# Edge block of a two-layer convolution kernel: the 512x512 fusion product as three float32r products of split operands

## The reference

```python
# layer 0
q, k, v = h @ wq.T, h @ wk.T, h @ wv.T            # 5x5 depthwise and 8x8 grouped convolutions of these are heads too
out = relu(q) . ((v, 1)^T relu(k)) / normaliser
x = batch_norm(proj_kernel @ out) + x
# layer 1, the edge block
E = [sobel, |laplace|, max of two |diagonals|, gradient]       # 3x3 stencils of x, four maps
feat = gelu(batch_norm(w_branch[e] @ E[e]))                     # 4 x 128 channels = 512
pooled = feat.mean(over pixels)
att = sigmoid(w_att2 @ gelu(w_att1 @ pooled))                   # one gate for each channel and image
z = w_fuse @ (feat * att) + b_fuse                              # the fusion product
zn = (z - mean_c(z)) / sqrt(var_c(z) + eps)
out = gelu(zn * ln_gamma + ln_beta) + x
```

## Time and profile before

| | us |
|---|---|
| median of 3 runs (lowest, highest) | 5002.34 (5001.51, 5005.30) |
| profiled execution: its time | 5005.31 |
| its span, first to last instruction | 5003.5 |
| TensorE busy (share) | 4718.9 (94%) |
| VectorE, ScalarE, GpSimd busy | 2836.0 (57%), 2173.3 (43%), 1253.1 (25%) |
| mean granted TensorE clock | 0.973 of full speed |
| matmuls of the fusion product (line 1142), busy | 454.4 in 1024 instructions |

### The profile page before, as it was taken

One profiled execution on the slowest core, in us unless ns is written; L12 is line 12 of the kernel. 1 busy time (PEld: TensorE's weight loads), 2 busy tenths in 40 slices (PEclk: granted clock), 3 DMA queues, 4 the chain that ended last, 5 costly groups with the idle time before them and its releaser, 6 DMA issues. The chain is left out here.

```text
span 5003.5 us, 68940 instructions
## 1 busy us (share of the span) xinstructions
PE 4718.9 (94%) x23784; PEld 3647.3 (73%) x23784; DVE 2836.0 (57%) x3927; ACT 2173.3 (43%) x3927; POOL 1253.1 (25%) x1030
## 2 busy tenths in 40 slices
PE   8999999999999999999999999589989998998968
PEld 7887888888878878888888788466546645654623
DVE  3354454454454444544544544279679949967975
ACT  3343343333333433333333333046556646646665
POOL 2341432433423414424333234000020021002003
PEclk9999999999999999999999999799999999999979
DMA  6675685676666756756766666767446646745613
GB/s 186 214 268 188 222 280 192 217 251 210 230 212 218 257 193 231 271 195 221 239 207 231 217 217 228 249 218 250 153 166 221 226 139 202 255 143 179 192 48 119
DMA packets 480190, 1044.92 MB, mean 209 GB/s; under 512 B 40368, under 2 KB 90160, under 8 KB 477616
## 3 DMA queue, kind: packets, MB, share of 16 engines
q1 hardware_dynamic: 479920, 1040.98, 62.1%
HBM read 665.02 MB, written 375.82 MB: 208 GB/s over the span
## 5 line engine op out<-in xcount | busy, mean ns | idle before, releaser
L786 POOL TENSOR_TENSOR toeplitz<-taps 128x512 f32<-128x512 f32 x768 | 918.5, 1224 | 993.9 <-PE bank L465 909.5
L465 PEld LDWEIGHTS bank<-toeplitz,columns 128*128 128x128 f32 x8192 | 954.4, 192 | 13.9
L465 PE MATMUL bank<-toeplitz,columns 128*128 128x128 f32 x8192 | 955.7, 275 | 0.0
L380 PE MATMUL bank<-x_hi,w_hi 128*128 128x512 f32 x1536 | 609.7, 397 | 15.5 <-DVE x_lo L635 15.5
L382 PE MATMUL bank<-x_lo,w_hi 128*128 128x512 f32 x1536 | 600.4, 391 | 0.0
L381 PE MATMUL bank<-x_hi,w_lo 128*128 128x512 f32 x1536 | 598.7, 390 | 0.0
L1451 POOL TENSOR_TENSOR centred<-centred,x_out 128x512 f32<-128x512 f32 x128 | 164.8, 1321 | 1708.2 <-ACT centred L1258 1708.2
L1116 PE MATMUL bank<-edge,w_branch 128*128 128x512 f32 x1024 | 480.4, 619 | 88.0 <-ACT edge L1209 88.0
L1102 PE MATMUL bank<-att_hi,w_proj_hi 128*128 128x512 f32 x1024 | 436.2, 426 | 62.2 <-DMA att_lo<-att_dram 50.5
L455 PE MATMUL bank<-loaded,toeplitz 128*128 128x256 f32 x2048 | 485.8, 379 | 7.8 <-POOL toeplitz L786 7.8
L635 DVE TENSOR_TENSOR x_lo<-x_sb,x_hi 128x1536 fp32r<-128x1536 f32 x128 | 251.9, 1968 | 399.6 <-ACT x_hi L511 399.6
(11 more groups left out here) (123 smaller groups left out, 6994.1 us busy)
## 6 DMA issues: line engine op xcount, KB each, us to landing
x_sb<-in_x_tiled SPq DMA_DIRECT2D x128, 1024.0 KB, 6.1
tiles_dram<-tiles SPq DMA_DIRECT2D x128, 867.0 KB, 7.0
loaded<-tiles_dram SPq DMA_DIRECT2D x256, 433.5 KB, 5.6
inverse<-inverse_dram SPq DMA_DIRECT2D x256, 256.0 KB, 7.9
att_dram<-out_hi SPq DMA_DIRECT2D x256, 256.0 KB, 4.2
att_dram<-out_lo SPq DMA_DIRECT2D x256, 256.0 KB, 5.9
att_hi<-att_dram SPq DMA_DIRECT2D x64, 1024.0 KB, 7.6
att_lo<-att_dram SPq DMA_DIRECT2D x64, 1024.0 KB, 10.0
```

The source lines that it names most:

```text
L380: nc.tensor.matmul(banks[t][:, :], wh, xh, start=(k == 0), stop=False)
L465: last = nc.tensor.matmul(bank[:, v * M:(v + 1) * M], columns[:, h % 2, t - T_K, v + b, a * HT:(a + TO) * HT], w[:, t, d, :], start=(d == ...
L786: last = nc.gpsimd.tensor_tensor(toeplitz[:, h % 2, t, :].rearrange("p (d o r) -> p d o r", o=HD, r=PL), tap, point, ALU.mult)
```

## The change

The fusion product is no longer made of float32 operands. `feat` is split, chunk by chunk, in a rounded part and a remainder: ScalarE rounds a 128x512 piece with a Copy into half 1 of `att_hi` (even chunks) or `att_lo` (odd chunks), four pieces a chunk (`round_feat`), VectorE subtracts for pieces 0 and 1 and GpSimd for pieces 2 and 3 (`split_feat`), writing `feat_lo` over `feat`. The gated weights are made as two parts: ScalarE writes `w_hi` with a Copy scaled by the gate, VectorE the remainder `w_lo`. For each of the four k, `fuse` now issues three float32r matmuls, wide x high, narrow x high and wide x low, instead of one float32 product. TensorE waits at m = 0 of each chunk for both subtracting engines. On SyncE, the load of half 1 of the next attention chunk moves from the drain to a place behind store 5 of the fusion, where it waits for the last fusion product of the image. GpSimd's residual additions of chunk j - 2 now stand behind its subtractions for chunk j + 1.

```diff
--- before.py
+++ after.py
@@ -832,7 +832,9 @@
         LAG = 3
         HALF = TILES // 2
         PIX = CR * W2
-        feat = sb("feat", [P, NE, N])
+        with nc.sbuf_tensor("feat", [P, NE, N], F32) as feat:
+            pass
+        feat_lo = ctx.enter_context(nc.sbuf_tensor("feat_lo", [P, NE, N], F32R))
         xb = sb("xb", [P, KT, XR * W2])
         work = sb("work", [P, 3, XR * W])
         with nc.sbuf_tensor("mean_w", [P, P], F32) as mean_w:
@@ -840,7 +842,7 @@
         sobel_h = sb("sobel_h", [P, 2, CR, W])
         sobel_v = sb("sobel_v", [P, 2, CR, W])
         lap_sq = sb("lap_sq", [P, 2, CR, W])
-        with nc.sbuf_tensor("w_image", [P, KT, C], F32) as w_image:
+        with nc.sbuf_tensor("w_image_hi", [P, KT, C], F32R) as w_hi, nc.sbuf_tensor("w_image_lo", [P, KT, C], F32R) as w_lo:
             pass
         edge = sb("edge", [P, 2, NE, CH])
         w_branch = sb("w_branch", [P, KT, NE, P])
@@ -894,7 +896,10 @@
         hidden_ready = sem("hidden_ready")
         gate_mm = sem("gate_mm")
         gate_ready = sem("gate_ready")
+        image_rounded = sem("image_rounded")
         image_ready = sem("image_ready")
+        feat_rounded = sem("feat_rounded")
+        feat_split = [sem("feat_split_v"), sem("feat_split_p")]
         fused = sem("fused")
         squared = sem("squared")
         squares_added = sem("squares_added")
@@ -910,6 +915,16 @@
         VAR_BANK, Z_BANKS = banks[0], banks[1:8]
         P_BANKS = (banks[5], banks[6], banks[7], banks[4])
         NORMED = START + KT
+
+        F_DVE, F_POOL = (0, 1), (2, 3)
+
+        def feat_hi(j, k):
+
+            return (att_hi, att_lo)[j % 2][:, 1, k, :]
+
+        def feat_of(tensor, j, k):
+
+            return tensor[:, k, j * CH:(j + 1) * CH]
 
         def v(name):
             return vec[:, VEC.index(name), :]
@@ -1041,8 +1056,9 @@
                     if p is not None:
                         sp.wait_ge(att_used, chunk(p, LAG))
                         load_att(p, LAG, 0)
-                        sp.wait_ge(projected, KT * chunk(p, LAG))
-                        load_att(p, LAG, 1)
+                        if b is None:
+                            sp.wait_ge(projected, KT * chunk(p, LAG))
+                            load_att(p, LAG, 1)
                         write_x2(p, LAG - 1, (LAG - 1) % 2)
                         load_rows(p, 0, 0, 16 * chunk(p, LAG))
                         for k in range(1, KT):
@@ -1062,6 +1078,9 @@
                                      centred[:, j % 2, :, :]).then_inc(stored[j % 2], 16)
                         if j + 2 < NCH:
                             load_out(b, j + 2)
+                        if j == NCH - 3 and not last:
+                            sp.wait_ge(fused, START + KT * NCH * b + KT * NCH)
+                            load_att(b + 1, LAG, 1)
 
                 schedule(start, step, drain, fusion)(sp)
                 for i in range(2):
@@ -1138,9 +1157,14 @@
                     n = KT * j + m
                     if n >= len(Z_BANKS):
                         pe.wait_ge(normed, NORMED + KT * NCH * b + n + 1 - len(Z_BANKS))
+                    if m == 0:
+                        for part in feat_split:
+                            pe.wait_ge(part, 2 * (NCH * b + j) + 2)
                     for k in range(KT):
-                        last = nc.tensor.matmul(Z_BANKS[n % len(Z_BANKS)][:, :], w_image[:, k, m * P:(m + 1) * P],
-                                                feat[:, k, j * CH:(j + 1) * CH], start=(k == 0), stop=(k == KT - 1))
+                        z, wide, narrow = Z_BANKS[n % len(Z_BANKS)][:, :], w_hi[:, k, m * P:(m + 1) * P], w_lo[:, k, m * P:(m + 1) * P]
+                        nc.tensor.matmul(z, wide, feat_hi(j, k), start=(k == 0), stop=False)
+                        nc.tensor.matmul(z, narrow, feat_hi(j, k), start=False, stop=False)
+                        last = nc.tensor.matmul(z, wide, feat_of(feat_lo, j, k), start=False, stop=(k == KT - 1))
                     last.then_inc(fused, 1)
 
                 def variance(b, j):
@@ -1258,18 +1282,36 @@
                         nc.scalar.activation(centred[:, j % 2, m, :], centred[:, j % 2, m, :], ACT.Gelu,
                                              scale=v("ln_gamma")[:, m:m + 1], bias=v("ln_beta")[:, m:m + 1]).then_inc(activated, 1)
 
+                def round_feat(b, j, ks):
+                    if j >= 2:
+                        act.wait_ge(fused, START + KT * NCH * b + KT * (j - 1))
+                    for k in ks:
+                        nc.scalar.activation(feat_hi(j, k), feat_of(feat, j, k), ACT.Copy).then_inc(feat_rounded, 1)
+
                 def fusion(b, last_image):
+                    act.wait_ge(projected, KT * (B * NCH if last_image else chunk(b + 1, LAG)))
+                    act.wait_ge(feat_ready, START + NE * NCH * b + NE * NCH)
+                    round_feat(b, 0, (0, 1))
                     act.wait_ge(hidden_mm, b + 1)
                     nc.scalar.activation(hidden[:, :], banks[1][0:HID, 0:1], ACT.Gelu, bias=b_att1[:, 0:1]).then_inc(hidden_ready, 1)
+                    round_feat(b, 0, (2, 3))
                     act.wait_ge(gate_mm, b + 1)
                     for m in range(KT):
                         nc.scalar.activation(gate[:, m:m + 1], banks[2][:, m:m + 1], ACT.Sigmoid,
                                              bias=v("b_att2")[:, m:m + 1]).then_inc(gate_ready, 1)
+                    for k in range(KT):
+                        act.wait_ge(gate_ready, KT * b + k + 1)
+                        nc.scalar.activation(w_hi[:, k, :], w_fuse[:, k, :], ACT.Copy, scale=gate[:, k:k + 1]
+                                             ).then_inc(image_rounded, 1)
                     for j in range(NCH + 2):
+                        if j == 0:
+                            round_feat(b, 1, (0, 1, 2, 3))
                         if 1 <= j <= NCH:
                             std(b, j - 1)
                         if j < NCH:
                             squares(b, j, 0)
+                            if 2 <= j + 1 < NCH:
+                                round_feat(b, j + 1, (0, 1, 2, 3))
                         if j >= 2:
                             activate(b, j - 2)
                         if j < NCH:
@@ -1406,6 +1448,11 @@
                     dve.wait_ge(squares_added, START + (KT - 1) * (NCH * b + j) + m - 1)
                     nc.vector.tensor_tensor(square[:, 0, :], square[:, 0, :], square[:, 1, :], ALU.add).then_inc(squares_added, 1)
 
+                def split_feat(b, j, k):
+                    dve.wait_ge(feat_rounded, KT * (NCH * b + j) + k + 1)
+                    nc.vector.tensor_tensor(feat_of(feat_lo, j, k), feat_of(feat, j, k), feat_hi(j, k).bitcast(F32),
+                                            ALU.subtract).then_inc(feat_split[0], 1)
+
                 def fusion(b, last_image):
                     dve.wait_ge(feat_ready, START + NE * NCH * b + NE * NCH)
                     nc.vector.tensor_reduce(row_sum[:, :], pool_sum[:, :, :], AX_X, ALU.add).then_inc(pool_summed, 1)
@@ -1414,10 +1461,15 @@
                     if not last_image:
                         add_residual(b + 1, LAG - 1, (LAG - 1) % 2, (2, 3))
                     nc.vector.memset(mean_w[:, :], 1.0 / C).then_inc(mean_w_set, 1)
-                    dve.wait_ge(gate_ready, KT * (b + 1))
+                    for k in F_DVE:
+                        split_feat(b, 0, k)
                     for k in range(KT):
-                        nc.vector.tensor_scalar(w_image[:, k, :], w_fuse[:, k, :], gate[:, k:k + 1], None,
-                                                ALU.mult).then_inc(image_ready, 1)
+                        dve.wait_ge(image_rounded, KT * b + k + 1)
+                        nc.vector.scalar_tensor_tensor(out=w_lo[:, k, :], in0=w_fuse[:, k, :], scalar=gate[:, k:k + 1],
+                                                       in1=w_hi[:, k, :].bitcast(F32), op0=ALU.mult, op1=ALU.subtract
+                                                       ).then_inc(image_ready, 1)
+                    for k in F_DVE:
+                        split_feat(b, 1, k)
                     for j in range(NCH + 1):
                         if j >= 1:
                             dve.wait_ge(std_ready, START + NCH * b + j)
@@ -1428,6 +1480,8 @@
                                 add_squares(b, j, m)
                             if j >= 1:
                                 norm(b, j - 1, m)
+                            if 2 <= j + 1 < NCH and m - 1 in F_DVE:
+                                split_feat(b, j + 1, m - 1)
 
                 schedule(start, step, drain, fusion)(dve)
 
@@ -1442,14 +1496,28 @@
                 def drain(p, b):
                     pass
 
+                def split_feat(b, j, k):
+                    pool.wait_ge(feat_rounded, KT * (NCH * b + j) + k + 1)
+                    nc.gpsimd.tensor_tensor(feat_of(feat_lo, j, k), feat_of(feat, j, k), feat_hi(j, k).bitcast(F32),
```

(25 more changed lines are left out.)

## The result

The changed kernel takes 5104.85 us (median of 4 runs, 5090.25 to 5112.74) against 5003.82 in the same rounds: ratio 1.0198, 95% interval 1.0175 to 1.0222. Forecast were 5111 and a range of 5056 to 5145. The profiled execution took 5105.15 us, its span is 5103.4.

What follows compares the result with a forecast made beforehand. It took a loop through ScalarE and VectorE to bound the fusion once the new work joined it. 4 x (23.8 an image + 3.4 at the start) = +109 us on 5005.3, 5114; median 5111, range 5056 to 5145.

Steps and rivals of the forecast that it cites:

- The bound and the loop: Fusion chunks: roundings and subtractions lengthen the loop through ScalarE and VectorE; a full chunk 18.7 us against 14.59 before.
- One image: Eight fusion chunks, half-clock phases and slow start summed to 145.4 us against 121.6, so +23.8 us an image.
- The clock: TensorE's pauses of 6 us before chunks 3 to 7 drop its clock, costing 1.8 us each, 9.0 an image.
- rival A: Fusions: loop right but clock does not fall, 5075 us, 12%; with GpSimd's meetings gone too, 5056, 5%.
- The start: Start of each fusion: roundings delay Gelu and Sigmoids, then weight roundings and remainder delay TensorE; together +3.4 us an image.
- The costs put at nothing: Attention load of half 1 stays covered, else up to 10 us an image; GpSimd's 2.6 us more a chunk also fits.
- C: Fusions: new work falls into waits, loop closes at the normalisation freeing the bank, 13.4 us a chunk; 4961 or 4917, 7%.
- B: Fusions heavier: half speed over all group 0 and variance, 5141, or whole GpSimd instructions waited for, 5145; 12%, both 4%.

Runs made afterwards that it cites:

- e5: The changed kernel with 18 more float32r matmuls on TensorE in each of chunks 1 to 6, filling its pause, results unchanged; 5069.0 us, ratio 1.0130.
- e3: The changed kernel with ScalarE's roundings moved ahead of the variance's root and VectorE's subtractions to the head of the chunk's work; 4965.5 us, ratio to before 0.9933.
- e8: The changed kernel with one float32 product of the rounded parts replacing the three float32r products, roundings and subtractions kept; 5116.5 us, ratio to before 1.0225.
- e7: The changed kernel with only wide x high left of the three products, all roundings and subtractions kept; 5019.4 us, ratio to before 1.0035.
- e6: The changed kernel with GpSimd's residual additions covering only 8 of 512 columns; 5074.2 us, ratio to before 1.0142.
- e9: e3 with ScalarE's square of group 1 ahead of the Gelus and chunk 0 of each image rounded by VectorE; 4970.1 us, ratio to before 0.9935.
- e12: e9 with GpSimd subtracting three of four pieces a chunk, but VectorE all four of chunk 0; 4959.5 us, ratio to before 0.9915.
- e2: The changed kernel with VectorE's two subtractions moved between group 0's normalisation and group 1's addition, roundings left in place; 5006.0 us, ratio to before 1.0002.

## Why the prediction was right

- **The bound and the loop:** right in place, and right in size for chunks 3 and 4. At full clock a chunk was forecast at 18.7 us; e5 shows 18.4 for these two, but 17.1 and 17.0 for chunks 5 and 6 (see "One image"). e3 takes roundings and subtractions out and lands at 13.2 to 13.7, forecast 13.4. e8 and e7 show that TensorE's own work decides little.
- **The clock:** five half-clock phases an image were right, and 1.8 us each a little low: e5 against the change gives 2.0 us for chunks 3, 4 and 5, 2.7 for chunk 6 (19.74 against 17.04) and 1.7 for chunk 7. That a pause of 2.88 us leaves the clock up, which rival A took from one row, does not hold: behind the same wait, two of the changed kernel's later images show the branch product at half clock, 5.40 us instead of 3.70:

```profile
3574.79 3.70 PE L1135 MATMUL bank<-edge,w_branch 128*128 128x512 f32 x8 [2.88 <-ACT edge L1233]
4029.17 5.40 PE L1135 MATMUL bank<-edge,w_branch 128*128 128x512 f32 x8 [2.87 <-ACT edge L1233]
```

- **The start:** +3.4 forecast; the first product comes 10.26 us behind the pooled mean instead of 6.77, +3.5, in the first three images (rows of 3581.93 and 3592.19), and +2.1 in the last, which has no projection ahead of it: 12.5 in all for 13.6. (The fusion products of before start at 3583.36, 4013.58, 4443.74 and 4865.43 us; the two middle ones were given wrongly, as 4009 and 4440.)
- **One image:** the mis-sized term. The stage grew by 94.6 us, the sum said 109. Less the start, that is 82 against 95, and the main part at fault is the root's table load of 1.28 us, which the sum has in the loop of chunk 1 and of chunks 3 to 7 from rows of one chunk. In later chunks it stands ahead of the wait for the variance, inside ScalarE's idle time. The changed kernel's timeline of ACT, chunk 4 and chunk 5:

```profile
3663.52 1.28 ACT L1267 ACT_TABLE_LOAD   x1 [6.65 <-PE bank L1175]
3664.81 0.69 ACT L1267 ACTIVATE work<-bank,per_channel 128x512 f32<-128x512 f32 x1
...
3679.20 1.28 ACT L1267 ACT_TABLE_LOAD   x1 [1.88 <-DVE centred L1442]
3683.91 0.69 ACT L1267 ACTIVATE work<-bank,per_channel 128x512 f32<-128x512 f32 x1 [3.43 <-PE bank L1175]
```

The trace of before had it as well, two chunks behind the one I read:

```profile
3660.79 1.28 ACT L1243 ACT_TABLE_LOAD   x1 [1.55 <-DVE centred L1400]
3662.68 0.69 ACT L1243 ACTIVATE work<-bank,per_channel 128x512 f32<-128x512 f32 x1 [0.61 <-PE bank L1151]
```

The order of instructions with their waits tells why. `std` has two waits, and no instruction of the program carries both. In chunks 5 to 7 the wait for the normalisation stands at the load, and the root has that for the variance; in chunks 3 and 4 the wait for the variance is an instruction of its own ahead of both. The idle times above fit: PE ends the one before the load in chunk 4, VectorE's `centred` the one in chunk 5.

```
L1266 ISA [waits var_ready]
L1267 ACT_TABLE_LOAD
L1267 ACTIVATE work<-bank,per_channel 128x512 [waits normed]
...
L1267 ACT_TABLE_LOAD [waits normed]
L1267 ACTIVATE work<-bank,per_channel 128x512 [waits var_ready]
```

Three such loads in each of three images and six in the last, whose rows all show it but the second root, which needs no load, and the final one, are 15 x 1.28 = 19 us too much in the sum. Some 0.3 us too little for each of 20 half-clock phases give 6 back: 95 - 19 + 6 = 82. That this meets the 82 to the microsecond is partly luck. The fusions themselves grew by 79.1 us (20.5, 21.8, 18.6 and 18.1), so other rows of the sum are 3 us too high, and 3.0 us lie behind the fusions, where the sum had nothing: 1.9 each ahead of the second and the third pooled mean (less 0.8 in the rest), 1.7 of them the branch product at half clock shown above.
- **The costs put at nothing** held: no wait for GpSimd's subtractions stands among those of the fusion product, and none for the attention load among those of TensorE after 3540 us.
- **The rivals:** C was not what happened, but its price for the loop at the bank was what e3 measured. The heavier half of B, a whole GpSimd instruction for each meeting, did not come either: in the change's loop the meetings cost 0.9 us a chunk (e6), as taken, on the addition and the first subtraction alone. Where both engines subtract side by side, VectorE's two take 3.43 us (e9), where four take 2.49 without GpSimd (e12), so each lost about 1.1 us, close to one GpSimd instruction (1.27 us). The Trainium skill's rule that the two block each other (SBUF — State Buffer, "Who interferes with whom") agrees with the traces in kind in both places; in size it is near only in e9.

The total also holds 5.3 us that lie before the first pooled mean (3581.93 against 3576.59), in code that is the same; single runs of before spread from 4991 to 5020. It was luck that they brought the total nearer to the forecast: of the 109 us foretold, 94.6 came in the stage.

## What to carry to other kernels

Before making a product cheaper, add up the loop through the other engines that its wait closes, over one period: here it was 14.0 us under 14.59 of TensorE's work, and 13.4 with the shorter group 0 in it, so at most 1.2 us a chunk could be had and not the 2.8 that TensorE saves. Some 5 us of new work put into the loop turned the gain into a loss. New work belongs where its engine waits anyway, ahead of the wait and not behind it; the same instructions moved there gave -0.7% instead of +2%. Read more than one period of a repeated stretch before multiplying it, since an instruction without a wait of its own can stand on either side of a wait.

## What was not expected of the hardware

- 432 more matmuls made the kernel faster (e5, -23 us in the stage): they filled pauses of 5 us, and group 0 behind them then took 2.9 us instead of 4.2 to 5.3.
- Pauses of 4.7 us and more in the fusions never left the clock up (20 of 20 in the change). Those of 1.6 to 2.2 us in e2 left it up 10 times in 20, and in the other ten the fall could come some matmuls behind the pause; pauses of 2.87 us before a branch product show both as well. So here the length of the last pause alone does not tell whether the clock falls.
- A VectorE instruction with two SBUF inputs ran up to 2.8 times as long beside GpSimd's (3.43 us for two in e9, 2.49 for four in e12).
